# One ScalarE copy of the negated maxima into both score slots of a group, in place of one copy per slot

## The reference

```python
xn = group_norm(x, 32 groups) * gn_w + gn_b
qkv = einsum('oc,bct->bot', qkv_w, xn) + qkv_b          # 3 * 64 rows per head
q, k, v = split(qkv)                                     # each (4 * 8 heads, 64, 2304)
weight = softmax(einsum('bct,bcs->bts', q * scale, k * scale))
a = einsum('bts,bcs->bct', weight, v)
out = xn + einsum('oc,bct->bot', proj_w, a) + proj_b
```

## Time and profile before

| what | value |
|---|---|
| median of three runs | 3720.25 us |
| the profiled execution | 3719.26 us, span 3717.6 us |
| TensorE busy | 3691.2 us (99%) |
| GpSimd busy | 3050.6 us (82%) |
| ScalarE busy | 2877.4 us (77%) |
| VectorE busy | 2101.8 us (57%) |
| granted TensorE clock | 0.999 of full speed |
| exponentials, L847 | 1728 of 809 ns |
| seed copies, L860 | 1728 of 819 ns |

### The profile page before, as it was taken

The page is one execution under the profiler, slowest core; times in us unless marked ns, Lnnn a source line. Parts: engine busy times, 40 slices in busy tenths (PEclk is TensorE's granted clock), DMA queues, the critical chain, the costliest instruction groups (busy, mean ns, idle before and its releaser), DMA issues.

```text
span 3717.6 us, 74814 instructions
## 1 busy us (share of the span) xinstructions
PE 3691.2 (99%) x30104; PEld 2271.1 (61%) x30104; DVE 2101.8 (57%) x2798; ACT 2877.4 (77%) x4091; POOL 3050.6 (82%) x1718
## 2 busy tenths in 40 slices
PE   8999999999999999999999999999999999999999
PEld 5565565656756565565675656556577565656657
DVE  6555556555555555655555555565555555555564
ACT  3777777888677777788767777788876777777886
POOL 1888888898389888888938898888874888989893
PEclk9999999999999999999999999999999999999999
DMA  2000012011400001211130000111123000000022
GB/s 82 21 17 26 23 33 74 21 57 34 152 20 22 18 24 32 74 35 43 51 134 25 18 23 17 56 51 46 41 77 103 23 20 23 21 20 20 19 83 96
DMA packets 132282, 165.03 MB, mean 44 GB/s; under 512 B 61792, under 2 KB 107872, under 8 KB 131424
## 3 DMA queue, kind: packets, MB, share of 16 engines
q1 hardware_dynamic: 131936, 160.26, 13.8%
HBM read 122.17 MB, written 38.04 MB: 43 GB/s over the span
## 4 chain that ended last, share of the span: by engine, by line
PE 97%; ACT 1%; DVE 1%; issue 0%; POOL 0%; DMA 0%; SPq 0%; ACTq 0%; POOLq 0%; DVEq 0%
PE oacc L661 31%; PE scores L637 24%; PE pool_bank L579 14%; PE aux_banks L601 13%; PE pool_bank L591 7%; PE scores L738 5%; PE pool_bank L624 2%; ACT probs L847 1%; PE scores L579 1%; ACT scores L860 0%; DVE stats L995 0%; DVE maxima L967 0%; POOL denom L1240 0%; PE scores L591 0%; DMA xn<-x 0%
## 5 line engine op out<-in xcount | busy, mean ns | idle before, releaser
L1240 POOL TENSOR_TENSOR denom<-denom,probs 128x768 f32<-128x768 f32 x1528 | 2797.5, 1831 | 373.4 <-ACT probs L847 192.0
L967 DVE TENSOR_REDUCE maxima<-aux_banks 128x2 f32<-128x512 f32 x1728 | 1657.5, 959 | 1450.6 <-PE aux_banks L601 1416.8
L847 ACT ACTIVATE probs<-scores 128x768 f32<-128x768 f32 x1728 | 1308.8, 809 | 656.5 <-PE scores L637 600.6
L860 ACT ACTIVATE scores<-seeds 128x768 f32<-128x768 f32 x1728 | 1339.5, 819 | 2.2 <-PE scores L645 1.5
L661 PE MATMUL oacc<-probs,vals 128*64 128x384 f32 x6912 | 1282.6, 492 | 0.0
L661 PEld LDWEIGHTS oacc<-probs,vals 128*64 128x64 f32 x6912 | 455.2, 136 | 519.7 <-issue 371.1
L601 PE MATMUL aux_banks<-k_hi,q_hi 64*128 64x512 f32 (+1 forms) x3456 | 680.9, 390 | 4.9 <-DVE maxima L967 4.9
L601 PEld LDWEIGHTS aux_banks<-k_hi,q_hi 64*128 64x128 f32 x3456 | 321.9, 183 | 531.4 <-issue 441.8
L637 PE MATMUL scores<-q_hi,k_hi 64*128 64x384 f32 x3456 | 591.6, 338 | 7.1 <-ACT scores L860 7.1
L637 PE MATMUL scores<-q_hi,k_lo 64*128 64x384 f32 x3456 | 587.0, 335 | 0.0
L637 PE MATMUL scores<-q_lo,k_hi 64*128 64x384 f32 x3456 | 586.7, 334 | 0.0
(11 more groups left out here) (96 smaller groups left out, 1558.3 us busy)
## 6 DMA issues: line engine op xcount, KB each, us to landing
seeds<-neg_rows SPq DMA_DIRECT2D x96, 384.0 KB, 3.5
xtile<-x SPq DMA_DIRECT2D x72, 384.0 KB, 3.2
att<-o_norm SPq DMA_DIRECT2D x96, 192.0 KB, 2.4
probs<-x SPq DMA_DIRECT2D x18, 768.0 KB, 4.6
out<-probs SPq DMA_DIRECT2D x18, 768.0 KB, 3.7
xtile<-att SPq DMA_DIRECT2D x12, 768.0 KB, 4.6
att_raw<-att SPq DMA_DIRECT2D x12, 768.0 KB, 6.3
neg_rows<-neg_cols SPq DMA_DIRECT2D x384, 0.8 KB
```

The costliest lines, as they stand in the source:

```text
L847: a(prob(s).rearrange("p (h n) -> p h n", n=N), scores[:, s % 2, :, 0:N], ACT.Exp, scale=SCALE).then_inc(probs_ready, 1)
L860: a(scores[:, s % 2, :, 0:N], seeds[blk % 2][:, :].rearrange("p (e n) -> p e n", n=N), ACT.Copy).then_inc(seeded, 1)
L967: v.tensor_reduce(maxima[:, :, qt, kc], aux_banks[:, :, 0:UNIT_KEYS[kc % 2]], AX.X, ALU.max)\
L1240: gp.tensor_tensor(acc, acc, prob(s), ALU.add).then_inc(added, 1)
```

## The change

One operation of ScalarE now copies the seeds into both slots of a group: 128 x 4 x 384 numbers written, the 128 x 768 of the seeds read twice. It is issued where the first of the two copies was, waits until both exponentials of the group before have ended (`probs_ready` up to step s, where the first copy waited only for the first), and counts `seeded` up by two at its end. At the start of batches 1 to 3 the first copy no longer comes two projection tiles before the end; both slots are seeded after the last tile is out.

```diff
             def seed(s, b, since=None):
 
                 blk = s // KT
-                if s % KT < 2:
+                if s % KT == 0:
                     act.wait_ge(seeds_in[blk % 2], 16 * (BLOCKS // 2 * b + blk // 2 + 1))
-                if s < 2:
+                if s == 0:
                     act.wait_ge(banks_opened, 1)
                     act.wait_ge(proj_saved, since)
                 else:
-                    act.wait_ge(probs_ready, PROBS_PRIMED + BSTEPS * b + s - 1)
-                a(scores[:, s % 2, :, 0:N], seeds[blk % 2][:, :].rearrange("p (e n) -> p e n", n=N),
-                  ACT.Copy).then_inc(seeded, 1)
+                    act.wait_ge(probs_ready, PROBS_PRIMED + BSTEPS * b + s)
+                a(scores[:, :, :, 0:N], seeds[blk % 2][:, :].rearrange("p (o e n) -> p o e n", o=1, n=N)
+                  .broadcast_to([128, GS, 2, N]), ACT.Copy).then_inc(seeded, GS)
...
                     for s in range(GS * i, GS * i + GS):
                         exponentials(s, b)
-                    for s in range(GS * i + 2, min(GS * i + 4, BSTEPS)):
-                        seed(s, b)
+                    if GS * (i + 1) < BSTEPS:
+                        seed(GS * (i + 1), b)
...
-                    if n == PJ - 3 and not last:
+                    if n == PJ - 1 and not last:
                         seed(0, b + 1, PRIMED + PJ * b + n + 1)
-                    if n == PJ - 1 and not last:
-                        seed(1, b + 1, PRIMED + PJ * b + n + 1)
...
-            for s in range(2):
-                seed(s, 0, PRIMED)
+            seed(0, 0, PRIMED)
```

## The result

The changed kernel takes 3907.18 us (median of 4 runs, 3905.11 to 3907.74), the kernel before 3719.95 us: a ratio of 1.0498, with a 95% interval of 1.0485 to 1.0511. That is 187 us more; 183 were forecast, and 3902 for the time. The profiled execution has a span of 3903.4 us against 3717.6.

What follows compares the result with a forecast made beforehand. TensorE was taken to bound the kernel, in a loop with ScalarE that the change lengthens to 4.04 us. Short groups 151, very short 28 and batch changes with program start 4 sum to 183 on 3719.3: 3902 us, range 3845 to 3955.

Steps and rivals of the forecast that it cites:

- What bounds: TensorE holds 97% of the chain; it hardly waits for seed copies, yet scores, exponentials and copies form one loop.
- The wait: Between the second exponential's end and the joint copy's start on ScalarE: 0.08 us, range 0.06 to 0.11.
- The copy: ScalarE's joint seed copy of 1536 columns: 1.47 us, range 1.43 to 1.55, against 1.55 for the pair.
- the loop: Scores, exponentials, wait, copy, next weight load: 4.04 us; a group takes the longer of this and TensorE's needs.
- Short, very short and long groups: Groups 3.70, 3.22 and 4.35 us apart (445, 34, 364 of them): growth of 151, 28 and 0 us.
- stays covered: ScalarE's other work behind the seeds, 0.49 to 1.03 us an instruction, fits the 0.98 before the next exponential.
- the groups near 4.0: 16 groups about 4.0 us apart before the change; growth under 1 us together.
- Change of batch: At the three batch changes both slots are seeded after the last tile: 1.2 us later each, 3.6 us.
- None of which reaches TensorE now: The exponentials' waits for GpSimd, 52.0 us in 57 times, do not reach TensorE and should shrink.
- No copy starts before the exponentials have ended: Tests the hidden-wait rival: copy starts 0.11 before the exponentials' end, loop 3.85, time 3811 us; chance 0.07.
- Fewer instructions: Rival: 69 us of ScalarE time saved makes the kernel faster, 3709 us; chance 0.02.
- The clock: Rival: TensorE's standstills in short groups bring 1.2 in place of 2.4 GHz, 1650 us more, 5550; chance 0.01.

Runs made afterwards that it cites:

- joint-signal run: Kernel before, still two copies started as early as before, but TensorE's first-step scores wait for both copies: 3844.07 us, ratio 1.0332.

## Why the prediction was right

- **What bounds.** That TensorE hardly waited before did not mean that the seed copy had much play: the copies' end stood 0.07 behind TensorE's start on the next group. This reading carried the forecast, and the joint-signal run shows it by itself.
- **What the close total owes to luck.** The short and very short groups carry 178 of the 186 us, and they are right by mechanism. The rest is right only in sum: 6.9 more at the square roots and 2.9 more at the starts of batches and of the program than forecast, against 4.3 and 2.6 less in long groups and in the one that had waited for GpSimd.
- **The wait.** Taken at 0.08, between 0.06 and 0.11; measured 0.092. The size was right, but for a reason that the prediction did not have: 32 ns are the wait as such, and 60 come from adding 2.
- **The copy.** Taken at 1.47, measured 1.455. The two small errors cancel, and the loop is 4.03 for 4.04.
- **Short, very short and long groups.** 151, 28 and 0 forecast; 151.1, 27.1 and about 0 measured.
- **Other work of ScalarE behind the seeds.** The step "stays covered" was mis-sized: it named instructions up to 1.03 us and left out the square root with its two table loads, 2.8 us. That is 6.9 us, 3.7 of them by the clock, and all that the groups near 4.0 grew beyond the forecast.
- **Change of batch.** Mis-sized: 3.6 forecast, 6.6 in the traces, or 6.1 with the first group behind each; the second wait of TensorE, one group later, was left out.
- **GpSimd.** "None of which reaches TensorE now" overlooked one wait of TensorE itself for the denominators, 3.2 us at its weight load, whose end brought 2.6 us. The stretch of the earlier trace rows holds it: 2.57 of the 3.6 us in which TensorE was idle there are this one standstill, and the granted clock of 1.00 in it says little on many short ones.
- **The rivals.** No copy starts before the exponentials have ended. Fewer instructions gained nothing against the kernel before; against two late copies with a joint signal they gave back 11 us. The clock did fall, not for the short waits of all groups, but behind three long ones: right in kind, and worth 3.7 us, not 1650. The bubble between ScalarE's instructions, which the Trainium skill describes under "The Read-Write Bubble" ("Advanced Engine Details and Errata"), agrees with these traces (1.55 for two copies, 1.455 for one of the same columns). It was not on the path of the kernel before, and came onto it only with the joint signal.

## What to carry to other kernels

Merging two instructions also merges their signals: whoever could start on the first half must now wait for the whole. Before doing it, find the loop that the instruction is part of, add up its pieces, and set the sum against the work of the engine that must not wait, for each kind of iteration and not on the mean; an iteration with 0.3 us of spare time pays nothing and its neighbour all. And count what interrupts the loop rarely, such as a table load: it was covered in part by the same play that the change uses up. When a total comes out close, compare it term by term: here four terms of 2 to 7 us, two up and two down, largely cancelled.

## What the runs showed of the hardware

- A ScalarE copy that waits and adds 1 started 32 ns after the exponential it waited for; one that adds 2 had a wait instruction of its own before it and started after 92 ns. So did a copy that adds 1 and waits for two things.
- ScalarE's copy from SBUF into PSUM costs 0.83 ns a column from 1088 to 2048 columns, written over four banks from a source read twice or more. The Trainium skill's formula ("ScalarE: Activation LUTs", "What ACT_TABLE_LOAD costs", 186 ns + 0.833 ns a column) gives 1466 for the 1455 measured.
- Two copies that wait on a finished exponential took 0.75 from start to start, two that overlap it 0.73.
- The granted clock fell to half behind a standstill of TensorE of 1.92 us, and stayed whole behind one of 0.99 us and hundreds of 0.3 to 0.7. It did not fall behind every long one: in the run whose `seeded` counts groups it fell at one of the three square roots, at two changes of batch and shortly after the stream's start. In the changed kernel it stayed whole behind 1.93 us at each of the three changes of batch, and in the kernel before behind the 2.57 us in which TensorE waited for GpSimd, while in the run with joint copies in long groups only it fell behind the same wait. What decides between the two is open.
